# Three transposes of the last stage done in pieces of 64 rows, and the values' projection in another bank

## The reference, cut to what matters

```python
def reference(...):
    x = L0_attn_x                                   # (2, 2048, 256)
    xn = _layernorm(x, axis=-1)
    s = _L0_attn_ref(xn, ...)                       # 16 heads, full attention, 2048 x 2048 per head
    g = _silu(_L0_ffn_ref(xn, ...))                 # two layers, below
    return x + s * g

def _layer(x, wqkv, qs, ksc, wo, lg, lb, w1, b1, w2, b2):   # run twice: DEPTH = 2
    h = shift_token(x)                              # second half of the features from the token before
    q, k, v = jnp.split(h @ wqkv, 3, axis=-1)       # 8 heads of 64, to_heads each
    q = l2norm(q) * qs
    k = l2norm(k) * ksc
    q, k = rotary_xpos(q, k)
    o = local_attention(q, k, v)                    # windows of 128 tokens, own window and the one before
    x = x + o @ wo
    h = shift_token(x)
    h = (h - h.mean(-1)) / jnp.sqrt(h.var(-1) + 1e-05) * lg + lb
    a, g = jnp.split(h @ w1 + b1, 2, axis=-1)
    return x + (a * gelu(g)) @ w2 + b2
```

## Time and profile before

| what | value |
|---|---|
| median of 3 runs | 2962.0 (2961.99 to 2963.34) |
| span of the profiled execution, first to last instruction | 2960.1 |
| its own time | not given by itself; the median is 1.9 above its span |
| busy share of PE, DVE, ACT, POOL | 99%, 79%, 77%, 38% |
| granted TensorE clock, mean | 0.994 |
| chain of waits that ended last, share on PE | 95% |
| PE in the last stage | some 1400 of the span |

### The profile page before, as it was taken

One profiled execution on the slowest core, in us unless ns is written; L12 is line 12 of the kernel. 1 busy time (PEld: TensorE's weight loads), 2 busy tenths in 40 slices (PEclk: granted clock), 3 DMA queues, 4 the chain that ended last, 5 costly groups with the idle time before them and its releaser, 6 DMA issues.

```text
span 2960.1 us, 97183 instructions
## 1 busy us (share of the span) xinstructions
PE 2919.8 (99%) x38016; PEld 1971.1 (67%) x38016; DVE 2325.1 (79%) x4219; ACT 2271.1 (77%) x4379; POOL 1111.0 (38%) x1835
## 2 busy tenths in 40 slices
PE   8999999999999999999989999999999999999998
PEld 4455555555555555555567777778777777877786
DVE  8888888888888888888856776667676667767665
ACT  4599999999999999999956666666666666666664
POOL 5421221111112211221245455555456554555554
PEclk9899999999999999999999999999999999999999
DMA  6631111111111111111121101111011111011110
GB/s 231 212 116 38 49 47 45 40 49 48 43 44 49 49 41 46 49 49 38 43 64 44 32 30 33 40 43 40 28 36 30 44 43 34 28 35 38 44 41 5
DMA packets 157206, 152.14 MB, mean 51 GB/s; under 512 B 17794, under 2 KB 130946, under 8 KB 156930
## 3 DMA queue, kind: packets, MB, share of 16 engines
q1 hardware_dynamic: 156930, 148.15, 16.0%
HBM read 89.37 MB, written 58.72 MB: 50 GB/s over the span
## 4 chain that ended last, share of the span: by engine, by line
PE 95%; DVE 3%; issue 1%; ACT 1%; SPq 0%; DMA 0%; POOL 0%; DVEq 0%; POOLq 0%; ACTq 0%
PE banks L1488 15%; PE banks L1450 15%; PE banks L1505 15%; PE banks L1690 11%; PE banks L1555 8%; PE banks L1703 6%; PE banks L1606 4%; PE banks L1645 4%; PE banks L1657 4%; PE banks L1566 4%; PE banks L1622 2%; PE banks L1578 1%; PE banks L1632 1%; PE banks L1587 1%; PE banks L1713 1%
## 5 line engine op out<-in xcount | busy, mean ns | idle before, releaser
L1146 DVE TENSOR_REDUCE pair_max<-banks 128x1 f32<-128x1024 f32 x1024 | 1219.7, 1222 | 145.5 <-PE banks L1450 115.8
L917 ACT ACTIVATE probs<-banks 128x512 f32<-128x512 f32 x2048 | 1158.7, 598 | 64.0 <-PE banks L1488 4.1
L1488 PE MATMUL banks<-q_aug,k_aug 98*32 98x512 bf16 x8192 | 1143.6, 381 | 0.8 <-ACT probs L917 0.4
L1450 PE MATMUL banks<-k_aug,q_aug 96*32 96x512 bf16 x8192 | 819.4, 382 | 5.3 <-ACT v_all L884 3.3
L1505 PE MATMUL banks<-probs,v_cur 128*32 128x256 f32 x8192 | 796.8, 379 | 0.2
L1488 PEld LDWEIGHTS banks<-q_aug,k_aug 98*32 98x32 bf16 x8192 | 391.7, 95 | 197.1 <-ACT probs L917 5.4
L1505 PEld LDWEIGHTS banks<-probs,v_cur 128*32 128x32 f32 x8192 | 366.8, 111 | 166.5 <-ACT acc_sb L898 0.8
L646 POOL TENSOR_SCALAR row_max<-pair_max 128x1 f32<-128x1 f32 x508 | 132.1, 283 | 886.5 <-DVE pair_max L1146 886.5
L1450 PEld LDWEIGHTS banks<-k_aug,q_aug 96*32 96x32 bf16 x8192 | 310.1, 97 | 218.2 <-DVE pair_max L1146 11.6
L1690 PEld LDWEIGHTS banks<-hnT,w_sb 128*128 128x128 f32 (+1 forms) x2816 | 320.2, 191 | 25.1 <-ACT hnT L997 25.1
L1690 PE MATMUL banks<-hnT,w_sb 128*128 128x128 f32 (+1 forms) x2816 | 332.4, 278 | 0.9 <-ACT hnT L997 0.9
(11 more groups left out here) (146 smaller groups left out, 4093.4 us busy)
## 6 DMA issues: line engine op xcount, KB each, us to landing
acc_scratch<-acc_sb SPq DMA_DIRECT2D x128, 256.0 KB, 2.4
heads_win<-acc_scratch SPq DMA_DIRECT2D x512, 64.0 KB
q_aug<-q_parts SPq DMA_DIRECT2D x192, 64.0 KB, 2.2
k_aug<-k_parts SPq DMA_DIRECT2D x192, 64.0 KB, 2.2
q_parts<-parts SPq DMA_DIRECT2D x16, 384.0 KB, 3.1
k_parts<-parts SPq DMA_DIRECT2D x16, 384.0 KB, 4.0
x_in<-in_x SPq DMA_DIRECT2D x10, 512.0 KB, 4.7
xT_scratch<-xnT SPq DMA_DIRECT2D x8, 512.0 KB, 5.2
```

The costliest lines, as they stand in the source:

```text
L917: nc.scalar.activation(probs[:, step % PRING, :], banks[:, ring(h, use), :], ACT.Exp, scale=SCALE).then_inc(prob_ready, 1)
L1146: nc.vector.tensor_reduce(pair_max[:, group % 2, q, half:half + 1], banks[:, 4 + 2 * (t % 2):6 + 2 * (t % 2), :], AX.XY, ALU.max).then_inc ...
L1450: last = nc.tensor.matmul(banks[m:m + CT, 4 + t % 4, :], q_aug[0:TERM_ROWS, b, q * P + m:q * P + m + CT], k_aug[0:TERM_ROWS, b, kq * BANK: ...
L1488: last = nc.tensor.matmul(banks[m:m + CT, ring(h, use), :], k_aug[0:AUG, b, kb * P + m:kb * P + m + CT], q_aug[0:AUG, b, qc * CHUNK:(qc + ...
```

## The change

In the last stage the transposes of keys, of queries and of the tokens ahead of the layer norm, 128x128 each, are replaced by two pieces each: rows 0 to 63 go to one bank and rows 64 to 127 to the next (`turn_rows`). Keys and queries share banks 1 and 2, keys in columns 0 to 255, queries in 256 to 511. They are now one function with one semaphore at its end. The tokens ahead of the layer norm go to columns 0 to 127 of the same two banks, and the values' projection goes to bank 3 in place of bank 2. ScalarE and VectorE read two banks where they read one. Three waits of TensorE are now followed by an increment of a semaphore of their own (`turns_seen`, `x1_seen`), as was so already at L1622 and L1678. The waits on `y_kept` and `sum_ready`, which say that banks 2 and 3 are free, change places.

```diff
@@ -945,21 +946,24 @@
                 l, b = parts_of(k)
                 act.wait_ge(v_ready, at(i, k))
                 act.wait_ge(v_carried, at(i, k))
-                nc.scalar.copy(vw[:, l, b, 1], banks[:, lanes(b) + 2, :]).then_inc(v_kept, 1)
+                nc.scalar.copy(vw[:, l, b, 1], banks[:, lanes(b) + 3, :]).then_inc(v_kept, 1)
 
             def keep_q(i, k):
 
                 b = k % B
-                act.wait_ge(qT_done, at(i, k))
-                nc.scalar.copy(qT[:, b], banks[:, lanes(b) + 3, :]).then_inc(qT_kept, 1)
+                act.wait_ge(qkT_done, at(i, k))
+                nc.scalar.copy(qT[:, b].rearrange("p j (r t) -> p r j t", r=2),
+                               banks[:, lanes(b) + 1:lanes(b) + 3, D:2 * D]
+                               .rearrange("p r (j t) -> p r j t", t=LD)).then_inc(qT_kept, 1)
 
             def keep_k(i, k):
 
                 l, b = parts_of(k)
-                act.wait_ge(kT_done, at(i, k))
+                act.wait_ge(qkT_done, at(i, k))
                 act.wait_ge(k_carried, at(i, k))
-                nc.scalar.copy(kT[:, l, b, :, WINDOW:],
-                               banks[:, lanes(b) + 1, :].rearrange("p (j t) -> p j t", t=WINDOW)).then_inc(kT_kept, 1)
+                nc.scalar.copy(kT[:, l, b, :, WINDOW:].rearrange("p j (r t) -> p r j t", r=2),
+                               banks[:, lanes(b) + 1:lanes(b) + 3, 0:D]
+                               .rearrange("p r (j t) -> p r j t", t=LD)).then_inc(kT_kept, 1)
 
             def exponentials(i, k, n):
 
@@ -1293,7 +1297,7 @@
             def normalise(i, k):
 
                 b = k % B
-                h_tok = banks[:, lanes(b) + 3, 0:D]
+                h_tok = banks[:, lanes(b) + 1:lanes(b) + 3, 0:P]
                 dve.wait_ge(h_done, at(i, k))
                 nc.vector.bn_stats(fstats[:, b], h_tok).then_inc(norm_step, 1)
                 dve.wait_ge(norm_step, at(i, k, 1, 2))
@@ -1302,8 +1306,9 @@
                 dve.wait_ge(norm_step, at(i, k, 2, 2))
                 nc.vector.tensor_scalar(fmv[:, b, 1:2], fmv[:, b, 1:2], LN_EPS, None, ALU.add).then_inc(var_done, 1)
                 dve.wait_ge(rstd_done, at(i, k))
-                nc.vector.tensor_scalar(hn[:, b], h_tok, fmv[:, b, 0:1], fmv[:, b, 1:2],
-                                        ALU.subtract, ALU.mult).then_inc(hn_ready, 1)
+                nc.vector.tensor_scalar(hn[:, b].rearrange("p (f r d) -> p r f d", f=2, r=2),
+                                        h_tok.rearrange("p r (f d) -> p r f d", f=2), fmv[:, b, 0:1],
+                                        fmv[:, b, 1:2], ALU.subtract, ALU.mult).then_inc(hn_ready, 1)
 
             def gate(i, k, part):
 
@@ -1561,32 +1566,35 @@
 
                 l, b = parts_of(k)
                 if l == 0:
-                    pe.wait_ge(y_kept, final_of(i, k) + (B * (k // ITEMS) + 1))
+                    pe.wait_ge(sum_ready, final_of(i, k) + (B * (k // ITEMS) + 1))
                 for f in range(2):
-                    last = nc.tensor.matmul(banks[:, lanes(b) + 2, :], xT[:, l, b, f, 1 - f:1 - f + WINDOW],
+                    last = nc.tensor.matmul(banks[:, lanes(b) + 3, :], xT[:, l, b, f, 1 - f:1 - f + WINDOW],
                                             wqkv_sb[:, l, f, 2 * INNER:], start=(f == 0), stop=(f == 1))
                 last.then_inc(v_ready, 1)
 
-            def transpose_q(i, k):
+            def turn_rows(b, at_col, tile):
+
+                for r in range(2):
+                    rows = slice(r * LD, (r + 1) * LD)
+                    last = nc.tensor.transpose(banks[:, lanes(b) + 1 + r, at_col:at_col + LD],
+                                               tile[rows], ident[rows, rows])
+                return last
+
+            def transpose_qk(i, k):
 
                 l, b = parts_of(k)
                 if l == 0:
-                    pe.wait_ge(sum_ready, final_of(i, k) + (B * (k // ITEMS) + 1))
+                    pe.wait_ge(y_kept, final_of(i, k) + (B * (k // ITEMS) + 1))
+                pe.wait_ge(k_turned, at(i, k))
+                nc.tensor.sem_inc(turns_seen, 1)
+                for j in range(NPAIR):
+                    turn_rows(b, j * LD, turned[:, b, 1, j * P:(j + 1) * P])
                 for j in range(NPAIR):
                     if j % 2 == 0:
                         pe.wait_ge(q_turned, at(i, k, j // 2 + 1, 2))
-                    last = nc.tensor.transpose(banks[:, lanes(b) + 3, j * P:(j + 1) * P],
-                                               turned[:, b, 0, j * P:(j + 1) * P], ident[:])
-                last.then_inc(qT_done, 1)
-
-            def transpose_k(i, k):
-
-                b = k % B
-                pe.wait_ge(k_turned, at(i, k))
-                for j in range(NPAIR):
-                    last = nc.tensor.transpose(banks[:, lanes(b) + 1, j * P:(j + 1) * P],
-                                               turned[:, b, 1, j * P:(j + 1) * P], ident[:])
-                last.then_inc(kT_done, 1)
+                        nc.tensor.sem_inc(turns_seen, 1)
+                    last = turn_rows(b, D + j * LD, turned[:, b, 0, j * P:(j + 1) * P])
+                last.then_inc(qkT_done, 1)
 
             def scores(i, k, n):
                 l, b = parts_of(k)
@@ -1663,9 +1671,9 @@
 
                 l, b = parts_of(k)
                 pe.wait_ge(x1_ready, at(i, k))
+                nc.tensor.sem_inc(x1_seen, 1)
                 for f in range(2):
-                    last = nc.tensor.transpose(banks[:, lanes(b) + 3, f * P:(f + 1) * P],
-                                               x1T[:, l, b, f, 1 - f:1 - f + WINDOW], ident[:])
+                    last = turn_rows(b, f * LD, x1T[:, l, b, f, 1 - f:1 - f + WINDOW])
                 last.then_inc(h_done, 1)
 
             def transpose_normed(i, k):
@@ -1725,8 +1733,7 @@
             nc.tensor.sem_inc(proj_done, B)
             for n in (1, 0):
                 project(0, 0, n)
-            transpose_k(0, 0)
-            transpose_q(0, 0)
+            transpose_qk(0, 0)
             project_v(0, 0)
             for n in range(2):
                 scores(0, 0, n)
@@ -1741,8 +1748,7 @@
                     project(i, k + 1, 0)
                 project_o(i, k)
                 if more:
-                    transpose_k(i, k + 1)
-                    transpose_q(i, k + 1)
+                    transpose_qk(i, k + 1)
                 transpose_h(i, k)
                 if more:
                     project_v(i, k + 1)
```

More of the change, by code:

```diff
@@ L280, in build @@
         k_turned = sem("k_turned")
-        qT_done = sem("qT_done")
-        kT_done = sem("kT_done")
+        qkT_done = sem("qkT_done")
+        turns_seen = sem("turns_seen")
+        x1_seen = sem("x1_seen")
         qT_kept = sem("qT_kept")
```

## The result

The changed kernel takes 2983.0 (median of 4 runs, 2981.95 to 2988.3) against 2962.0 before: a ratio of 1.0074, 95% interval 1.006 to 1.0089. It is 21 slower. The forecast had the direction and half of the size (2972.7), and its range ended at 2979. The profiled run, the longest, took 2988.3 with a span of 2986.5.

The account below looks back on a forecast made before the run. TensorE, busy for 99% of the span, was taken as the bound, with two waits on VectorE; 63 passes each 0.17 longer add 10.7 to 2960.1, giving 2970.8, plus 1.9 for the runs' median, 2972.7. Range 2966.5 to 2979.

Parts of the forecast that it names:

- VectorE's run: Queries' projection to the sum ahead of the layer norm: unbroken, still ending at 2263.53 however fast keys and queries are transposed.
- the two stalls: TensorE's waits for the turned queries' second half (ready 2263.19) and for `x1_ready` (2263.53), both hanging on VectorE.
- the return to full width: Ahead of the values' projection: load 0.15 after the last pair, and bare, so the projection starts 0.17 later.
- the less even spacing of the pieces: Tokens' pieces behind their wait: if they come out less even, the projection is 0.20 later instead of 0.17.
- One sign: Last output product's start to the values' projection's first product: 1.51 in place of 1.34.
- the cover: Ahead of the tokens' pieces: the wait for `x1_ready` hides keys' and queries' costs, all over 0.16 before it ends.
- the first change of width: Output projection to keys' pieces: 0.09 and a bare load of 0.06, 0.15 a pass if not covered.
- The rivals without a drain: Width changes ahead of values' projection cost nothing: 0.10 a pass earlier, 2955.7 (0.05); with slower signal, 2960.1 to 2963.3 (0.10).
- by the tally: `x1_ready` earlier too, ten pairs running through, both drains paid: projection 0.28 earlier, 17.6 in all, 2944.4; chance 0.03.
- The rival with a new wait on the shared banks: Copies of keys and queries or swapped waits hold TensorE: 0.5 a pass, 31, 2993; more than 2978 had chance 0.05.
- the sum, 63 x 0.17: Later start of the values' projection in 63 passes of the last stage: 10.7 in all, giving 2972.7.
- From there to the next pass's queries everything waits for TensorE or is ready: After L1678's product, which moves from 2266.64 to 2266.81: the 0.17 is handed on whole each pass.

Follow-up runs that it names:

- e2_keys_queries: Changed kernel with the tokens ahead of the layer norm transposed at full width again, keys and queries still in pieces: 2962.9, ratio 1.0007 to the kernel before.
- e8_short_turn_before: Kernel before, full transposes, VectorE adding only 8 of every 256 columns of the turned queries: 2953.4 against 2961.7, passes of 21.83 and 23.00.
- e7_increment: Kernel before with one semaphore increment behind TensorE's wait for `x1_ready`, transposes at full width: 2966.6 against 2961.7, ratio 1.0015.
- e12_queries_full: Changed kernel with the queries' four transposes at full width, keys and tokens in pieces: 2975.6 against 2962.9, ratio 1.0045.
- e9_short_turn_after: Changed kernel, VectorE adding only 8 of every 256 columns of turned queries, 196 increments at TensorE's start: 2979.2 against 2962.9, passes of 21.88 and 23.05.
- e5_shifted_more: Changed kernel with 196 increments of an unused semaphore at the start of TensorE's stream: 2995.6 against 2961.7, start delay included.
- e13_gpsimd_quarter: Kernel before, full transposes, GpSimd adding the last 128 columns of the turned queries, VectorE the first 384 in one instruction: 2957.8 against 2961.9, ratio 0.9987.

## Why the prediction was right and wrong

**Right: the bound.** VectorE's run ends when it did, 0.12 ahead of the pieces' load as reckoned, and faster transposes of keys and queries bring nothing (`e2_keys_queries`). `e8_short_turn_before` gives 0.14 a pass when the run is shorter: that is what the two stalls read from the earlier trace rows cost.

**Right: the return to full width.** The step "0.15 from the last pair to the projection's load, which is bare" holds: in the changed kernel the last piece starts at 2261.57 and the projection's load comes at 2261.72.

```profile
2261.57 0.22 PE L1579 MATMUL banks<-ident,x1T 64*128 64x64 f32 x1
2261.73 0.70 PE L1571 MATMUL banks<-wqkv_sb,xT 128*128 128x512 f32 x1
```

The last piece itself starts 0.14 behind the pieces' load and not 0.12: that is the less even spacing of the pieces, which the prediction named with 0.20 a pass. One sign has to be read otherwise than it was written. A product whose load is bare is recorded as starting with that load, so the projection's first product stands 1.43 behind the last output product (2260.30) and not 1.51; the second stands at 2262.26, 1.96 behind the same place, where before it was 1.77 (2264.29 after 2262.52). That is the 0.19. Between its 0.17 and its 0.20, 0.185 was measured, a term of 11.7 in place of 10.7. That the increment is a part of it (0.065, the signal's 0.12 for 0.05) and that the cover holds for the first change of width are shown by `e7_increment` and `e12_queries_full`. The rivals without a drain and by the tally fall; the tally would not have come even with VectorE out of the way, since the pieces are then still 0.05 behind (`e9_short_turn_after`). The rival with a new wait on the shared banks, which stood for times above 2978, falls too: the second copy is done at 2261.98 + 0.59 = 2262.57, and the scores' load comes 1.07 later.

```profile
2261.98 0.59 ACT L955 COPY qT<-banks 128x512 f32<-128x512 f32 x1
...
2263.64 0.73 PEld L1614 LDWEIGHTS banks<-kT,qT 64*128 64x128 f32 x8 [0.76 <-issue]
```

**Wrong: the sum has no term for code.** The step that failed is the sum, 63 x 0.17, and the sentence it rests on, "From there to the next pass's queries everything waits for TensorE or is ready": that sentence goes through the data's waits only, and the sum puts the fetching of code at nothing without a reason. Ninety-six more instructions in TensorE's loop made it fetch code again at the jump back. That cost 13.2 in the profiled run; in the median it is the other 9.3, by difference. Moved to where no code is fetched again, the same kernel costs its steady passes alone (`e5_shifted_more`). The page of the kernel before had the row for the question (fetches, MB):

```profile
q8 instruction: 211, 3.46, 0.5%
```

That is 16 KB a fetch, and none of them falls into the steady windows, hence a loop that is kept on the engine. In the Trainium skill, Runtime: NRT & Kernel Launch, Instruction fetch mechanics, it is stated that TensorE has 128 KiB for code, refilled in blocks of 16 KiB, and that a taken branch whose target lies outside the current window of two such blocks has to fetch it first. By that rule the jump back was worth a rival. The traces agree with the size of the blocks and with a stand at the jump. They don't agree with two blocks as the window that is kept: in the profiles loops of 1640 to 1716 instructions, over six blocks by the 256 instructions that the section gives to one, ran all windows after the first without any fetch.

What the runs show of it is this. Unmoved, loops of 1640, 1660, 1696 and 1716 instructions are kept in their profiles, one of 1736 is fetched again after some windows, and one of some 1816 at each jump back. Moved by 128, 1640 is hit in some executions and 1736 at each jump; moved by 196, 1736 is free; moved by 256, it is as unmoved or nearly (one stand for two). One reading fits all of them: what counts is where the loop's end lies, counted from the start of the block in which it begins, with a stretch of uncertain outcome beyond that of the loop of 1716 (1736, and 1640 + 128 = 1768, lie in it, 1816 does not; whether 1716 lies just outside hangs on the one long run of `e2_keys_queries`). That this limit is the eighth block's start is an estimate, worked out with `e5_shifted_more`, and not shown. What makes the outcome in that stretch differ from window to window is open, and how many stands the timed runs of the changed kernel had isn't known: one profile shows two, in the longest run.

## What to carry to other kernels

Where an engine waits for another one's unbroken run, find what is last to be ready there before making the work ahead of it faster; here the gain was on VectorE, by giving a quarter of one addition away. Then look again at who waits: merging two additions into one there took back half of what could be had. A pair of pieces of 64 rows took 0.06 to 0.07 where a full transpose took 0.11, but as an island between full-width products it brought nothing here: the way back cost 0.15 and a bare load of 0.11. That pieces pay in a stretch which stands at that division anyway is not shown. Count an engine's instructions in a loop before adding to it, and look at the row of the instruction queue after: a loop that was kept may no longer be, by its length or by its place.

## What the runs showed of the hardware

- Twenty instructions more in a loop (1716 to 1736) began the stands of 4.1 and 4.5 at its jump, and 128 harmless instructions at the program's start turned two stands into one at each of 14 jumps (113 more than the changed kernel unmoved, of which some 12 is the later start). After a stand TensorE's granted clock was 0.79 over 8. Each stand came with nine more fetches of 16 KB.
- An increment behind a wait on TensorE delayed the load by 0.065 (`e7_increment`). A second wait at the same place did about the same without an increment (0.11 to 0.12 for 0.06, `e13_gpsimd_quarter`). Among dense products 44 increments per item made a pass 1.5 longer, 0.034 each.
- GpSimd's addition of two tensors took 0.97 for 256 columns and 0.83 for 128. By these two, an estimate, some 0.7 of it does not depend on the columns.
